# Dense stages of a four-layer graph network: LayerNorm statistics in five groups of five tiles instead of one pass, and the accumulators cleared by ScalarE instead of GpSimd

## The chip, the cores and the metric

The program runs on one core of one Trainium2 chip. The metric is the device time of one execution in microseconds (us), lower is better. A profile is one further execution, taken by the hardware profiler.

## The reference

Four residual layers on 3125 nodes with 256 features and 50000 edges. Each layer normalizes the rows of `x`, applies ReLU, and feeds the result to one layer kind:

```python
h = jnp.maximum(_layernorm(x, axis=-1), 0.0)
x = x + _L0_gnn_ref(h, edge_weight, src, dst)          # h @ (256x256 product of rotations)
h = jnp.maximum(_layernorm(x, axis=-1), 0.0)
x = x + _L1_gnn_ref(h, edge_index, edge_attr_64, ...)  # q, k, v, skip projections, edge softmax, sums by target
h = jnp.maximum(_layernorm(x, axis=-1), 0.0)
x = x + _L2_gnn_ref(h, edge_index, ...)                # GAT: h @ W0.T, scores, edge softmax, elu
h = jnp.maximum(_layernorm(x, axis=-1), 0.0)
x = x + _L3_gnn_ref(h, edge_index, edge_attr_64, ...)  # GAT block with a closing layernorm
```

`_layernorm` is `(x - m) / sqrt(v + 1e-5)` over the 256 features of a row.

## The kernel before

The nodes lie in 25 tiles of 125 rows (`P` = 125, `NT` = 25, `D` = 256). `X` holds all of `x` in SBUF, and `acc` (125 x 25 x 272 numbers, 6800 a partition) holds the sums that the edge stages add up by target node. The program is a row of stages, each a `phase` that ends in a barrier of all engines: constants, the list of rotations, the rotations, dense 0, the graph stage, dense 1, blend (edges of layer 1), dense 2, attend 2 and its end, dense 3, attend 3, final. Only `dense_phase` is changed; it runs four times, for layers 0 to 3. The profile calls the tiles of all four `d_...`.

A dense stage has two parts, in this order.

**Statistics.** VectorE (DVE) runs a loop over all 25 tiles: a `bn_stats` (L946) for each. In layer 2 (`settle=True`) two more instructions stand ahead of it for each tile, which divide the tile's sums in `acc` by their weights (L942) and add them to `X` (L944). Then seven small instructions turn the statistics of all 25 tiles at once into a variance (L950 to L956), ScalarE (ACT) takes one square root for all (L1009), and two more on DVE make `rstd` and `nb` (L958, L959), which release the rest by the semaphore `ready`.

**Products.** A loop over five groups of `U` = 5 tiles, the first of them peeled off (`peeled`). ACT writes the five normalized tiles `hn` (L1017), then copies each tile's transpose from PSUM to `ht` (L1022). TensorE (PE) transposes a tile (`turn`, L1033, two matmuls) and multiplies the tile before it by the weights (`multiply`, L1044: 256 columns in layer 0, 1024 in layer 1, 272 in layers 2 and 3); its order is turn 0, turn 1, product 0, turn 2, product 1, turn 3, product 2, turn 4, product 3, product 4. DVE moves each product out of PSUM (L970; L972 to L977; L980 to L987). SyncE stores the tables to HBM. ACT may not write `hn` of a tile before DVE has finished the same tile of the group before (`evac`); only layer 3 reads `hn` on DVE (L980).

GpSimd (POOL) clears `acc` with one `memset` of 6800 columns (L1003), in layer 2 after the last tile has been settled. Each engine runs its own instructions strictly in their order.

Of the kernel before, what the change touches and what calls it, by code (L numbers as in the profile page):

```python
# [13 lines left out]
ALU = mybir.AluOpType  # L14
# [3 lines left out]
P = 125  # L18
# [5 lines left out]
D = 256  # L24
# [51 lines left out]
def peeled(eng, count, body):  # L76

    body(0)
    with eng.Fori(1, count) as i:
        body(i)  # L80

# [826 lines left out]
def dense_phase(nc, con, layer, X, acc, ntab, weight, width, bias, tables, base=None, settle=False, loads=()):  # L908

    U = 5  # L910
    with phase(nc) as ph:
# [8 lines left out]
        inv = sb("inv", [P, NT, H]) if settle else None  # L920
        banks = -(-width // 512)
# [5 lines left out]
        cleared, lined, slanted, settled, brought = sem("cleared"), sem("lined"), sem("slanted"), sem("settled"), sem("brought")  # L927
        stores = 2 if layer == 1 else len(tables)
        with nc.Block() as block:
            @block.vector  # L930
            def _(dve):
                if settle:
# [5 lines left out]
                with dve.Fori(0, NT) as n:  # L938
                    x = X[:, bass.ds(n, 1), :].rearrange("p a d -> p (a d)")
                    if settle:  # L940
                        m = acc[:, bass.ds(n, 1), 0:MW].rearrange("p a (h c) -> p (a h) c", h=H)[:, :, 0:C]
                        dve.tensor_tensor(m, m, inv[:, bass.ds(n, 1), :].rearrange("p a h -> p (a h)").unsqueeze(2).to_broadcast([P, H, C]), ALU.mult).then_inc(settled, 1)  # L942
                        dve.wait_ge(settled, n * 2 + 3)
                        dve.tensor_tensor(x.rearrange("p (h c) -> p h c", h=H), x.rearrange("p (h c) -> p h c", h=H), m, ALU.add).then_inc(settled, 1)  # L944
                        dve.wait_ge(settled, n * 2 + 4)
                    dve.bn_stats(st[:, bass.ds(n, 1), :].rearrange("p a s -> p (a s)"), x).then_inc(dv, 1)  # L946
                dve.wait_ge(dv, NT)
                c = Tally(dve, dv, NT)
                me, mo = st[:, :, 1], st[:, :, 4]
                c.up(dve.tensor_tensor(mean[:], me, mo, ALU.add))  # L950
                c.up(dve.tensor_tensor(dif[:], me, mo, ALU.subtract))
                c.then(dve.tensor_tensor(var[:], st[:, :, 2], st[:, :, 5], ALU.add))
# [8 lines left out]
                def body(i):  # L961
                    for u in range(U):
# [3 lines left out]
                        if stores and not isinstance(i, int):  # L966
                            dve.wait_ge(stored[u], 16 * stores * i)
# [1135 lines left out]
```

## Time and profile before

| what | value |
|---|---|
| median of 3 runs | 3375.41 us (3375.38 to 3379.78) |
| time of the profiled execution | 3375.93 us |
| its span (first to last instruction) | 3374.2 us |
| PE, DVE, ACT, POOL busy | 75%, 69%, 50%, 46% of the span |
| mean granted clock of PE | 0.857 of full speed |

The time of the profiled execution is 1.7 us more than its span; what is said of the span holds for the time. Since all stages are kept apart by barriers, a stage's length counts whole, and the shares of the page, which are averages over stages with quite different limits, say little about the dense ones. They are read stage by stage.

### The profile page before, as it was taken

The numbers are of one execution on the slowest core, as the hardware profiler recorded it, in microseconds if no ns is written. First come the engines' busy times: TensorE is split into PE (matmuls) and PEld (weight loads), VectorE is DVE, ScalarE is ACT, GpSimd is POOL, SyncE is SP. The second block draws the span as 40 slices with busy tenths as digits, with TensorE's granted clock in tenths as the row PEclk, the third lists the DMA queues.
The fourth block names the chain that finished last, engine by engine and source line by source line (L and its number), as shares of the span: only waits on it lengthen the run. The fifth ranks groups of instructions, "written<-read, shape, count | busy, mean of one in ns | idle before, by whom it ended". The sixth has DMA issues, their size and how long they took to land. (4 is left out here: it accounts for less than half of the span.)

```text
span 3374.2 us, 57511 instructions
## 1 busy us (share of the span) xinstructions
PE 2535.7 (75%) x13060; PEld 1918.1 (57%) x13061; DVE 2319.7 (69%) x5727; ACT 1680.8 (50%) x4017; POOL 1550.9 (46%) x1759
## 2 busy tenths in 40 slices
PE   2999997357999999999995358888881368787870
PEld 1888886223666666666664246666660256666650
DVE  4888886464677787777775636766778547666677
ACT  1666664111454555545552246666661356666651
POOL 1333332101454555445551077777750177777740
PEclk9999998678999999999997767877785768888785
DMA  2100000213555556555651155555532255555521
GB/s 72 19 8 10 10 8 7 64 53 103 152 156 151 158 153 162 154 151 156 162 156 35 36 145 139 139 140 138 138 96 36 59 154 141 140 143 140 142 74 38
DMA packets 186285, 348.91 MB, mean 103 GB/s; under 512 B 74085, under 2 KB 116478, under 8 KB 185951
## 3 DMA queue, kind: packets, MB, share of 16 engines
q0 software_dynamic: 83520, 249.39, 29.0%
q1 hardware_dynamic: 102685, 98.62, 10.2%
q8 instruction: 30, 0.49, 0.1%
q14 instruction: 50, 0.41, 0.0%
HBM read 325.45 MB, written 22.44 MB: 103 GB/s over the span
## 5 line engine op out<-in xcount | busy, mean ns | idle before, releaser
L1626 POOL DMA_INDIRECT t_rows<-table_h,t_istage x896 | 853.5, 953 | 266.1 <-issue 247.1
L1212 POOL DMA_INDIRECT b_rows<-table_kv,b_istage x448 | 480.5, 1072 | 389.5 <-PE b_pso L1349 266.7
L1713 PE MATMUL t_pso<-t_rows,t_hot 125*125 125x272 f32 (+1 forms) x1792 | 588.1, 483 | 68.8 <-DVE t_rows L1752 30.5
L1713 PEld LDWEIGHTS t_pso<-t_rows,t_hot 125*125 125x125 f32 x1792 | 395.7, 232 | 164.5 <-issue 73.4
L1274 ACT COPY b_asked<-b_psq 125x512 f32<-125x512 f32 x224 | 131.1, 585 | 470.3 <-PE b_psq L1313 470.3
L1752 DVE TENSOR_TENSOR t_rows<-t_rows,t_psm 125x1056 f32<-125x1056 f32 x224 | 276.9, 1236 | 33.0 <-issue 32.9
L1699 PE MATMUL t_pss<-node_scores,t_hot_t 125*125 x1792 | 269.4, 281 | 33.5 <-ACT t_hot_t L1657 31.1
L1699 PEld LDWEIGHTS t_pss<-node_scores,t_hot_t 125*125 125x125 f32 x1792 | 263.7, 227 | 49.2 <-issue 43.7
L1664 ACT ACTIVATE t_hot<-con_iota,g_dstl 125x125 f32<-125x125 f32 x896 | 280.3, 384 | 0.0
L1762 DVE TENSOR_TENSOR acc<-acc,t_pso 125x272 f32 (+1 forms) x448 | 192.6, 430 | 114.7 <-DVE acc L1762 70.0
L1313 PE MATMUL b_psq<-queries,b_hot_t 125*125 x896 | 235.5, 386 | 43.9 <-issue 26.2
L1329 PE MATMUL b_psk<-b_rows,con_ident 125*125 125x256 f32 x896 | 257.9, 411 | 0.0
L1349 PE MATMUL b_pso<-b_rows,b_hot 125*125 125x264 f32 x896 | 239.1, 412 | 24.8 <-DVE b_rows L1428 24.5
L1406 DVE TENSOR_TENSOR b_rows<-b_psk,b_asked 125x1024 f32<-125x1024 f32 x112 | 136.5, 1218 | 150.5 <-ACT b_asked L1274 150.5
L1655 ACT ACTIVATE t_hot_t<-t_places,t_minus 125x500 f32<-125x500 bf16 x224 | 156.5, 699 | 142.2 <-PE t_pss L1699 110.3
L1033 PE MATMUL d_pst<-con_ident,d_hn 125*128 125x125 f32 x200 | 37.9, 290 | 224.5 <-ACT d_hn L1017 224.5
L1313 PEld LDWEIGHTS b_psq<-queries,b_hot_t 125*125 125x125 f32 x896 | 162.7, 189 | 74.8 <-issue 50.9
L1329 PEld LDWEIGHTS b_psk<-b_rows,con_ident 125*125 125x125 f32 x896 | 152.5, 190 | 90.2 <-issue 77.0
L1349 PEld LDWEIGHTS b_pso<-b_rows,b_hot 125*125 125x125 f32 x896 | 165.2, 194 | 56.6 <-issue 28.9
L1326 PE MATMUL b_psk<-we,b_attr 64*125 64x256 f32 x896 | 160.4, 435 | 22.2 <-DMA b_rows<-table_kv,b_istage 14.5
L1044 PE MATMUL d_pso<-wt,d_ht 128*125 128x512 f32 (+1 forms) x400 | 150.8, 518 | 25.5 <-ACT d_ht L1022 25.5
L1033 PEld LDWEIGHTS d_pst<-con_ident,d_hn 125*128 125x128 f32 x200 | 28.1, 151 | 245.2 <-ACT d_hn L1017 227.0
(392 smaller groups left out, 5194.3 us busy)
## 6 DMA issues: line engine op xcount, KB each, us to landing
t_places<-targets SPq DMA_DIRECT2D x56, 488.3 KB
t_rows<-table_h,t_istage POOLq DMA_INDIRECT x896, 3.0
b_attr<-in_attr_t SPq DMA_DIRECT2D x224, 62.5 KB
b_places<-targets SPq DMA_DIRECT2D x28, 488.3 KB
b_rows<-table_kv,b_istage POOLq DMA_INDIRECT x448, 5.2
table_h<-d_stage SPq DMA_DIRECT2D x50, 132.8 KB
t_flag<-flags SPq DMA_DIRECT2D x56, 62.5 KB
table_kv<-d_moved SPq DMA_DIRECT2D x25, 128.9 KB
```

Source lines behind the costliest of these rows:

```text
L1212: pool.indirect_dma_start(out=rows[:, h, s, :], out_offset=None, in_=table, in_offset=bass.IndirectOffsetOnAxis(ap=istage[:, h, s:s + 1], ...
L1313: mm = pe.matmul(ps_q[0:P, w * D:(w + 1) * D], hot_t[:, b % 2, v * PAIR + w, :], q, start=True, stop=True)
L1326: pe.matmul(to(v * PAIR + w), attr[half, b, w * P:(w + 1) * P], we[half], start=True, stop=False)
L1329: mm = pe.matmul(to(u), ident[0:P, 0:P], rows[0:P, h, b * G + u, 0:D], start=False, stop=True)
L1349: mm = pe.matmul(ps_o[0:P, at:at + MW], hot[:, h, b * G + u, :], rows[0:P, h, b * G + u, D:WIDE], start=u % PAIR == 0, stop=u % PAIR == PA ...
L1626: pool.indirect_dma_start(out=rows[:, r, s, :], out_offset=None, in_=table, in_offset=bass.IndirectOffsetOnAxis(ap=istage[:, r, s:s + 1], ...
L1655: act.activation(x, places[:, r, b * G * P:(b + 1) * G * P], ACT.Abs, bias=minus[0:P, :]).then_inc(broad, 1)
L1664: act.activation(hot[:, r, b * G + u, :], con["iota"][0:P, 0:P], ACT.Abs, scale=-1.0, bias=g["dstl"][:, bass.ds(n * G + u, 1)]).then_inc(d ...
L1699: mm = pe.matmul(expanded[:, b * G + u], hot_t[:, b % 2, u, :], ntab[:, bass.ds(ts[u // PAIR], 1), 0:nw].rearrange("p a d -> p (a d)"), st ...
L1713: mm = pe.matmul(ps_o[b % 2][0:P, at:at + mw], hot[:, r, b * G + u, :], rows[0:P, r, b * G + u, 0:mw], start=u % PAIR == 0, stop=u % PAIR ...
L1752: dve.tensor_tensor(v, v, weight[:, b * G:(b + 1) * G].unsqueeze(3).to_broadcast([P, G, H, HW]), ALU.mult).then_inc(mset, 1)
L1762: dve.tensor_tensor(row, row, ps_o[b % 2][0:P, v * 512:v * 512 + mw], ALU.add).then_inc(added, 1)
```

## The change

The statistics are taken group by group. On DVE `measure(g)` holds the five `bn_stats` of a group (in layer 2 with their two instructions of settling) and the seven small instructions, now over 5 columns instead of 25; `level(g)` holds the two that follow the square root. DVE runs `measure(0)` and `level(0)` ahead of the loop. In the loop, group `i` begins with `measure(i + 1)`, then finishes its tile 0, then `level(i + 1)`, then tiles 1 to 4. ACT takes the square root of group `i + 1` (`root`) between its second and third copy of group `i`. The wait of ACT on `evac` ahead of `hn` stays in layer 3 alone. POOL clears a small tile `zeros` (1360 columns) at the start, and ACT copies it over the group's five tiles of `acc` (`clear`) at the end of each group. The last group is peeled off as well on DVE and ACT (`tapered`).

```diff
+def tapered(eng, count, body):
+    body(0)
+    with eng.Fori(1, count - 1) as i:
+        body(i)
+    body(count - 1)
...
+                def measure(g):
+                    c = Tally(dve, dv, g * PER)
+                    for u in range(U):
...
+                        c.up(dve.bn_stats(st[:, bass.ds(n, 1), :].rearrange("p a s -> p (a s)"), x))
...
+                    dve.tensor_scalar(var[:, s], var[:, s], EPS, None, ALU.add).then_inc(spread, 1)
...
+                def body(i):
+                    if not last(i):
+                        measure(i + 1)
+                    finish(i, 0)
+                    if not last(i):
+                        level(i + 1)
+                    for u in range(1, U):
+                        finish(i, u)
...
-                with dve.Fori(0, NT) as n:
...
-                dve.wait_ge(ready, 1)
-                peeled(dve, NT // U, body)
+                measure(0)
+                level(0)
+                tapered(dve, GROUPS, body)
...
-                    if settle:
-                        pool_wait(pool, settled, 2 * NT + 2)
-                    pool.memset(acc[:], 0.0).then_inc(cleared, 1)
-                    pool.wait_ge(cleared, 1)
+                    pool.memset(zeros[:], 0.0).then_inc(empty, 1)
+                    pool.wait_ge(empty, 1)
...
+                def root(g):
+                    s = bass.ds(g * U, U)
+                    act.wait_ge(spread, g + 1)
+                    act.activation(dif[:, s], var[:, s], ACT.Sqrt).then_inc(rooted, 1)
+
+                def clear(g):
+
+                    act.copy(acc[:, bass.ds(g * U, U), :].rearrange("p n x -> p (n x)"), zeros[:].rearrange("p n x -> p (n x)")).then_inc(cleared, 1)
...
                 def body(i):
+                    act.wait_ge(ready, i + 1)
                     for u in range(U):
                         n = i * U + u
-                        if not isinstance(i, int):
+                        if layer == 3 and not opening(i):
                             act.wait_ge(evac, n - U + 1)
...
+                    copied(i, 0)
+                    copied(i, 1)
+                    if not last(i):
+                        root(i + 1)
+                    for u in range(2, U):
+                        copied(i, u)
+                    if layer:
+                        clear(i)
```

What stands on ACT in the first, peeled group of layer 1, before (the square root of all tiles, the five normalized tiles, the five copies of transposes, then the loop's branch):

```order
L1009 ACTIVATE d_dif<-d_var 125x25
L1017 ACTIVATE d_hn<-x,d_nb,d_rstd 125x256 x5
L1022 COPY d_ht<-d_pst 128x250 x5
L79 UNCONDITIONAL_BRANCH
L79 ISA
```

And what stands there in the changed kernel:

```order
L1062 ACTIVATE d_hn<-x,d_nb,d_rstd 125x256 x5
L1054 COPY d_ht<-d_pst 128x250 x2
L1046 ACTIVATE d_dif<-d_var 125x5
L1054 COPY d_ht<-d_pst 128x250 x3
L1050 COPY acc<-d_zeros 125x1360
```

The square root of the next group stands between the second and the third copy of this one, and the copy of zeros between the fifth copy and the next group's `hn`. The table for the square root is loaded once ahead of each dense stage in both kernels.

What stands on DVE at the start of the first group of layer 2, before (end of the statistics of all tiles, then tile 0 and the start of tile 1 of the group):

```order
L956 TENSOR_SCALAR d_var<-d_var 125x25
L958 RECIPROCAL d_rstd<-d_dif 125x25
L959 SCALAR_TENSOR_TENSOR d_nb<-d_mean,d_rstd 125x25
L991 MEMSET d_stage 125x5x8
L981 COPY node_scores<-d_pso 125x8
L982 COPY d_stage<-d_pso 125x8
L985 TENSOR_TENSOR node_scores<-d_pso,d_stage 125x8
L987 COPY d_stage<-d_pso 125x8x32
L981 COPY node_scores<-d_pso 125x8
```

And in the changed kernel, from the last tile that `measure(1)` settles to the start of tile 1:

```order
L960 TENSOR_TENSOR acc<-acc,d_inv 125x8x32
L962 TENSOR_TENSOR x<-x,acc 125x256
L964 BN_STATS d_st<-x 125x6
L968 TENSOR_TENSOR d_mean<-d_st 125x5
L969 TENSOR_TENSOR d_dif<-d_st 125x5
L970 TENSOR_TENSOR d_var<-d_st 125x5
L971 TENSOR_SCALAR d_mean<-d_mean 125x5
L972 SCALAR_TENSOR_TENSOR d_dif<-d_dif 125x5
L973 SCALAR_TENSOR_TENSOR d_var<-d_var,d_dif 125x5
L974 TENSOR_SCALAR d_var<-d_var 125x5
L1002 COPY node_scores<-d_pso 125x8
L1003 COPY d_stage<-d_pso 125x8
```

Four more such triples stand ahead of the first row. The statistics of the next group are now in front of tile 0 of this one, and the `MEMSET` of `d_stage` stands ahead of `measure(0)`.

## Rows read from the trace of the kernel before

**Rows 1.** The page: span.

```profile
span 3374.2 us, 57511 instructions
```

**Rows 2.** Windows: the products of layers 0, 1; statistics and products of 2; products of 3.

```profile
core 0: us, PE busy (x) PEld busy (x) DVE busy (x) ACT busy (x) POOL busy (x), PEclk, DMA share, GB/s
...
580.97:618.95 37.98, 30.42 (x150) 24.45 (x150) 10.54 (x25) 21.18 (x50) 0.00 (x0) 0.92 0.00 0
...
710.22:818.97 108.75, 96.61 (x250) 43.49 (x250) 54.81 (x101) 21.74 (x50) 0.00 (x0) 0.96 0.18 58
1846.92:1896.69 49.77, 0.00 (x0) 0.00 (x0) 40.02 (x87) 1.47 (x2) 5.76 (x1) 0.50 0.03 10
1896.69:1939.93 43.24, 33.24 (x150) 25.13 (x150) 18.72 (x102) 21.75 (x50) 0.00 (x0) 0.91 0.24 71
...
2641.23:2684.36 43.13, 33.15 (x150) 24.92 (x150) 22.70 (x101) 21.75 (x50) 0.00 (x0) 0.92 0.23 70
```

**Rows 3.** Timeline of layer 1's statistics: start us, us, engine, line, operation.

```profile
695.91 12.25 DVE L946 BATCH_NORM_STATS2 d_st<-x  x25 [2.96 <-PEq L73]
708.19 0.20 DVE L950 TENSOR_TENSOR d_mean<-d_st 125x25 f32<-125x25 f32 x1
...
709.18 0.18 DVE L956 TENSOR_SCALAR d_var<-d_var 125x25 f32<-125x25 f32 x1
...
710.22 2.56 ACT L1017 ACTIVATE d_hn<-x,d_nb,d_rstd 125x256 f32<-125x256 f32 x5 [0.60 <-DVE d_nb L959]
```

**Rows 4.** Layer 2's 25 settling instructions (ns, first and last start).

```profile
L942 DVE TENSOR_TENSOR acc<-acc,d_inv x25: 425/425/426, 1849.2 to 1888.5; - x25
```

**Rows 5.** Timeline of layer 2's clearing of acc on POOL and DVE beside it.

```profile
1889.57 5.76 POOL L1003 MEMSET acc<- 125x6800 f32 x1 [102.12 <-DVE x L944]
...
1890.52 4.85 DVE L953 TENSOR_SCALAR d_mean<-d_mean 125x25 f32<-125x25 f32 x1
```

**Rows 6.** Timeline of one group of layer 0; brackets: idle before, releaser.

```profile
596.12 2.62 ACT L1017 ACTIVATE d_hn<-x,d_nb,d_rstd 125x256 f32 x5
...
597.50 0.42 DVE L970 TENSOR_TENSOR x<-x,d_pso 125x256 f32 x1 [0.44 <-PE d_pso L1044]
598.65 0.61 ACT L1022 COPY d_ht<-d_pst 128x250 f32<-128x250 f32 x2
...
599.13 1.12 PE L1044 MATMUL d_pso<-MT,d_ht 128*125 128x256 f32 x4 [1.35 <-ACT d_ht L1022]
...
600.50 0.37 ACT L1022 COPY d_ht<-d_pst 128x250 f32<-128x250 f32 x1 [1.24 <-PE d_pst L1033]
...
603.12 2.63 ACT L1017 ACTIVATE d_hn<-x,d_nb,d_rstd 125x256 f32 x5
```

**Rows 7.** Timeline of layer 1: where a group's first product begins, two groups.

```profile
773.74 0.59 PE L1033 MATMUL d_pst<-con_ident,d_hn 125*128 125x125 f32 x4
...
776.37 3.69 PE L1044 MATMUL d_pso<-wt,d_ht 128*125 128x512 f32 x8 [2.04 <-ACT d_ht L1022]
...
796.93 5.39 PE L1044 MATMUL d_pso<-wt,d_ht 128*125 128x512 f32 x8 [2.04 <-ACT d_ht L1022]
```

**Rows 8.** Timeline of layer 2: its first product, and the last group's start.

```profile
1899.56 2.18 PE L1044 MATMUL d_pso<-wt,d_ht 128*125 128x272 f32 x4 [1.04 <-ACT d_ht L1022]
...
1929.41 2.29 ACT L1017 ACTIVATE d_hn<-x,d_nb,d_rstd 125x256 f32 x4
```

**Rows 9.** Timeline of layer 3, around the start of one group.

```profile
2657.70 0.37 ACT L1022 COPY d_ht<-d_pst 128x250 f32<-128x250 f32 x1 [0.95 <-PE d_pst L1033]
...
2660.14 0.41 DVE L987 COPY d_stage<-d_pso 125x256 f32<-125x256 f32 x1
...
2661.29 0.61 ACT L1022 COPY d_ht<-d_pst 128x250 f32<-128x250 f32 x2
2661.76 1.18 PE L1044 MATMUL d_pso<-wt,d_ht 128*125 128x272 f32 x4 [1.83 <-ACT d_ht L1022]
```

**Rows 10.** ACT's groups by form: busy us, mean ns, idle before and releaser.

```profile
L1274 ACT COPY b_asked<-b_psq 125x512 f32<-125x512 f32 x224 | 131.1, 585 | 470.3 <-PE b_psq L1313 470.3
...
L1022 ACT COPY d_ht<-d_pst 128x250 f32<-128x250 f32 x100 | 34.3, 363 | 103.5 <-PE d_pst L1033 103.5
```

More of the change, by code:

```diff
@@ L910, in dense_phase @@
     U = 5
+    GROUPS = NT // U
     with phase(nc) as ph:
@@ L920, in dense_phase @@
         inv = sb("inv", [P, NT, H]) if settle else None
+        zeros = sb("zeros", [P, U, RW]) if layer else None
         banks = -(-width // 512)
@@ L926, in dense_phase, with last @@
         stored = [sem(f"stored{u}") for u in range(U)]
-        cleared, lined, slanted, settled, brought = sem("cleared"), sem("lined"), sem("slanted"), sem("settled"), sem("brought")
+        empty, cleared, lined, slanted, settled, brought, put = (
+            sem(n) for n in ("empty", "cleared", "lined", "slanted", "settled", "brought", "put"))
         stores = 2 if layer == 1 else len(tables)
+        def last(i):
+            return isinstance(i, int) and i == GROUPS - 1
         with nc.Block() as block:
@@ L937, in _ @@
                     dve.wait_ge(con["x_brought"], 16)
-                with dve.Fori(0, NT) as n:
-                    x = X[:, bass.ds(n, 1), :].rearrange("p a d -> p (a d)")
-                    if settle:
[L941 to L952, printed above, removed]
-                c.up(dve.tensor_scalar(mean[:], mean[:], 0.5, None, ALU.mult))
-                c.then(dve.scalar_tensor_tensor(dif[:], dif[:], 0.25, dif[:], ALU.mult, ALU.mult))
@@ L1018, in body @@
                                        bias=nb[:, bass.ds(n, 1)], scale=rstd[:, bass.ds(n, 1)]).then_inc(hset, 1)
-                    for u in range(U):
-                        n = i * U + u
-                        act.wait_ge(tset, n + 1)
-                        act.copy(ht[:, u], ps_t[u % 2][:, 0:2 * P].rearrange("p (a m) -> p a m", a=2)).then_inc(tcopied, 1)
-                peeled(act, NT // U, body)
+                    copied(i, 0)
[6 more added lines that the diff above has]
+                        clear(i)
+                root(0)
+                if layer:
+                    act.wait_ge(empty, 1)
+                tapered(act, GROUPS, body)
             @block.tensor
@@ L1070, in body @@
                                 sp.dma_start(tables[0][bass.ds(n * P, P), :], stage[:, u, :]).then_inc(stored[u], 16)
-                    peeled(sp, NT // U, body)
+                    peeled(sp, GROUPS, body)
                     for u in range(U):
-                        sp.wait_ge(stored[u], 16 * stores * (NT // U))
+                        sp.wait_ge(stored[u], 16 * stores * GROUPS)
                     if loads:
```

93 lines of the change are left out of this document (55 added, 38 removed).

## The prediction

> **What bounds the kernel now.** I read the page first for the span of 3374.2 us [rows 1], then a table of windows over the dense stages [rows 2], then the timeline inside them. The stages stand behind one another with barriers between, so what a dense stage gets shorter, the whole gets shorter. A dense stage has two parts that never overlap. In the statistics only DVE works: in layer 1 they last from 695.91 to 710.22, 14.3 us [rows 3], and in layers 0 and 3 the same length (the pattern repeats three times); in layer 2, where each tile is settled as well, 49.8 us with no matmul at all [rows 2]. In the products PE is busy 89% of layer 1's 108.75 us, so PE bounds that one, and 77 to 80% in the others, where nobody is full: DVE has 10.5 of 38.0 us in layer 0, 18.7 of 43.2 in layer 2, 22.7 of 43.1 in layer 3 [rows 2]. There the round through ACT bounds: five `hn`, two copies, PE's first product, the third copy behind it [rows 6].
>
> **What is taken off the front.** One `bn_stats` takes 0.49 us (12.28 us for 25, from 695.91 to 708.19), and from there to the first `hn` it is 2.03 us [rows 3]. With 5 columns instead of 25 I take 1.85 for the latter (an estimate, bounds 1.6 and 2.03). A group's statistics then cost 5 x 0.49 + 1.85 = 4.3 us, and the first `hn` comes 10.0 us earlier in layers 0, 1 and 3. In layer 2 a tile costs 1.64 us (39.3 us over 24 steps [rows 4]), 20 tiles 32.7 us. There POOL's clearing of `acc` also held a DVE `TENSOR_SCALAR` for 4.85 us, to the end of the 5.76 us memset [rows 5], where it takes 0.18 otherwise [rows 3]; that 4.7 us goes too, and with the 0.2 of narrower columns it makes 37.6 us.
>
> Against it: the new clearing of `zeros` is a fifth as wide, 5.76 x 1360/6800 = 1.15 us, and begins with the stage, while DVE now begins layers 1 and 3 with its own memset, and layer 2 with a `TENSOR_SCALAR`, the form that was held. I charge 0.8 us in each of the three (bounds 0 and 1.15; for the memset no row shows it). Front: -10.0 - 9.2 - 36.8 - 9.2 = **-65.2 us**.
>
> **What comes back in the products.** The seven small instructions of `measure` took 1.2 us up to the release of the root [rows 3]; in the loop their waits stand against registers, for which I add 0.25. A slice is then 5 x 0.49 + 1.45 = 3.9 us, and 5 x 1.64 + 1.45 = 9.65 in layer 2 (bounds 0.3 less, 0.6 more). Four slices run in each layer. DVE has room for them, but ACT's square root waits for the slice, and the third, fourth and fifth copies of the group ahead are queued behind it; PE's products 2 to 4 wait for those, and DVE's finishing of them. The first slice of layers 0, 1 and 3 begins with the first `hn` and is done ahead of the third copy.
>
> *Layer 0.* Count from an `hn` start, T = 596.12 [rows 6]. DVE finishes the group before at T + 1.8; the slice ends at T + 5.7. The third copy, at T + 4.4 before, comes at T + 6.15. Its product follows 0.48 later (598.65 to 599.13) and the fifth copy 1.37 behind that product's start (599.13 to 600.50), T + 8.0, the next `hn` at T + 8.45, against 7.0. Three groups pay 1.45: **+4.35**, net -5.65.
>
> *Layer 1.* PE's transposes begin at 773.74 and the first product at 776.37, because ACT's `hn` of tiles 3 and 4 waited on DVE by `evac`. Without that wait `hn` is ready long before, and the product follows transpose and copy by 0.42 + 0.48 = 0.9 us instead of 2.63 [rows 7]: -1.73 in four rounds, -6.9. One of these rounds met half the clock after the 2.04 us of idle and took 5.39 instead of 3.69 us [rows 7]; I take that 1.7 as saved as well. The slice is hidden: DVE needs 54.81/25 = 2.2 us a tile [rows 2], 11 and 4.9 for slice and level, of 18.8 us a round. So is the clearing, which ACT does while PE multiplies. **-8.6**, net -17.8.
>
> *Layer 2.* The slice of 9.65 us is longer than the round, which was (1929.41 - 1896.69)/4 = 8.2 us [rows 2, 8]. Count from the end of a slice, M. Root and third copy follow at M + 0.45, the product at M + 0.9, and DVE has finished tile 4 at M + 5.3 if PE runs at full clock (1.18 us a product [rows 9]). But PE has then idled some 6 us, and a gap of 2 us was already enough once for half the clock [rows 7]. At the lower level a product takes 2.18 [rows 8], the three and the transpose between end 3.1 us later, M + 8.4. Then the next slice. A round is 18.05 us (14.95 at full clock). I take the lower level for all rounds but the first. From the first `hn`: 9.4 (first slice) + 5.3 + 9.65 = 24.3, two rounds make 60.4; from the end of the last slice to the last `hn` 5.45 (fifth copy at M + 3.6, clearing, start), and from there 10.0 (10.5 before [rows 2, 8], without the wait on `evac`). 75.8 us against 43.2 [rows 2]: **+32.6**, net -4.2.
>
> The Trainium skill, TensorE: Matmul & The Clock Gate, section HAM oscillation, says that a loop whose bursts of matmuls are separated by long enough waits restarts every burst at the lower clock. This speaks against the change in layer 2. The trace agrees by the 5.39 us product; with the rule left out layer 2 would be the full-clock case.
>
> *Layer 3.* The wait on `evac` stays. The clearing is a copy of 1360 columns: the rows have 363 ns for 250 and 585 for 512 columns [rows 10], 0.85 ns a column, so 1.3 us, with start 1.35 (bounds 1.1 and 1.6). Count from the fifth copy, C = 2657.70 [rows 9]. The first copy of the next group stood at C + 3.6, now at C + 0.45 + 1.35 + 2.6 = C + 4.4. DVE finishes at C + 2.85, the slice ends at C + 6.75, the third copy comes at C + 7.2 and the fifth at C + 9.05, a round, against 7.9. With tile 4 finishing 0.35 later, the next two rounds pay 1.45. 1.15 + 2 x 1.45 + 0.8 for the last group: **+4.9**, net -4.3.
>
> The Trainium skill, ScalarE: Activation LUTs, section Rules for kernel authors, budgets 0.3 us plus 0.83 ns an element, which would make the clearing an estimated 1.43 us. By it layer 3 would pay a few tenths more.
>
> Sum: -5.65 - 17.8 - 4.2 - 4.3 = -31.95 us, on the profiled execution's own 3375.93: 3344.0. The median of the runs is 0.5 lower: **3343.5 us**.
>
> **The rivals.**
> 1. *Layer 2 keeps the full clock* (0.20). Rounds of 14.95: 24.3 + 29.9 + 4.2 + 10.0 = 68.4, 7.4 us less: 3336. For it: in layers 0, 2 and 3 gaps of 1.4 and 1.8 us left the clock alone [rows 6, 9]. Against: 6 us is three times longer than any gap inside a round today.
> 2. *The held root costs nothing in layers 0 and 3* (0.08), if the slices run shorter than I have them: 4.35 + 4.05 less, 3335. Against: the third copy is due at T + 4.4 and DVE has only 2.6 us ahead of it.
> 3. *Slices are dearer* (0.09): a dozen instructions and more, some with waits on registers, 1.5 us more in each of the nine that count: 3357.
> 4. *Slower: the lower clock spreads* (0.03). The root's wait opens a second gap in each round of layers 0 and 3, and if PE drops there and in layer 1 as well, 40 tiles pay about 1.0 us (2.18 less 1.18) and 20 pay 1.7 [rows 7 to 9]: +74, 3417. It decides from 19 of layer 1's 20 tiles on. Against: these gaps are 1 to 2 us, and layer 1's becomes shorter.
> 5. *No change* (0.05): the front is taken off but the stage's end is set by something not in my rows, such as the stores of the tables, and the time stays within 0.2% of 3375.4. Against: DMA is busy 0.18 to 0.24 in the products [rows 2].
>
> My forecast has 0.55, with a range of its own of 3338 to 3350.
>
> **How the numbers follow.** Low end: rival 1 with clearing and memsets free, 3331. High end: slices at 0.6 more in nine places (+5.4), the collision at its full 1.15 (+1), half clock once more in layer 1 (+1.7) and in a few tiles of layer 3 (+4): 3356. A measurement of this kernel can tell about 0.2%, 6.8 us, from no change. All but rivals 4 and 5 lie below 3368.6: faster 0.92, the same 0.05, slower 0.03.
>
> **What would show it.** First `hn` 4.3 us after the first `bn_stats` in layers 0, 1 and 3, and some 10.4 after the division in layer 2. ACT's square root waiting 2 to 3 us for DVE in layers 0 and 3 and about 8 in layer 2, with the third copy right behind it. Products in layer 1 18.8 us a round, no wait of ACT on DVE. In layer 2 rounds of 18 us, products of 2.1 us at half clock behind the gap. A copy of zeros of 1.3 us. Wrong would make it: rounds in layer 2 over 20 us, DVE held by POOL for more than a microsecond, or gaps between the instructions of a slice.

## The result and the profile after

The changed kernel takes 3328.9 us (median of 4 runs, 3326.4 to 3330.5); the kernel before, run beside it, 3377.6 us. The ratio is 0.9856, 95% interval 0.9844 to 0.9868: 48.7 us faster, where I had forecast 32 us, with 3331 as the low end of the range. One execution of the kernel e7 below took 6150.0 us; it is left out of e7's ratio, and nothing on record says why it took that long. The profiled execution of after took 3328.8 us. Its page begins:

```profile
span 3327.0 us, 57408 instructions
```

That is 47.2 us under [rows 1]. Windows over the dense stages of after (columns as in [rows 2]): the products of layers 0 and 1, the first statistics of layer 2, the products of layers 2 and 3.

```profile
570.25:610.45 40.20, 31.69 (x150) 24.85 (x150) 22.48 (x81) 20.90 (x54) 0.00 (x0) 0.92 0.00 1
690.23:790.39 100.16, 94.91 (x250) 42.86 (x250) 66.14 (x156) 27.53 (x59) 0.00 (x0) 0.97 0.20 63
1823.70:1833.79 10.09, 0.00 (x0) 0.00 (x0) 9.18 (x28) 1.45 (x2) 1.19 (x1) 0.50 0.15 52
1833.79:1902.93 69.14, 40.74 (x150) 29.49 (x150) 47.12 (x197) 26.61 (x59) 0.00 (x0) 0.76 0.15 44
2590.61:2636.99 46.38, 36.29 (x150) 25.56 (x150) 34.09 (x156) 27.14 (x59) 0.00 (x0) 0.89 0.22 65
```

Set against [rows 2, 3] they give the table that the rest of this text uses, in us. "Front" is first DVE instruction to first `hn`, "products" from there to DVE's last instruction; a stage's front before is 14.3 in layers 0, 1 and 3.

| layer | front, forecast | front, measured | products, forecast | products, measured | net, forecast | net, measured |
|---|---|---|---|---|---|---|
| 0 | -10.0 | -10.9 | +4.35 | +2.2 | -5.65 | -8.6 |
| 1 | -9.2 | -10.8 | -8.6 | -8.6 | -17.8 | -19.4 |
| 2 | -36.8 | -39.7 | +32.6 | +25.9 | -4.2 | -13.8 |
| 3 | -9.2 | -10.8 | +4.9 | +3.3 | -4.3 | -7.6 |
| sum | -65.2 | -72.2 | +33.25 | +22.8 | -31.95 | -49.4 |

The other stages give back 2.2 us, which makes the 47.2. Most of that is in the stages that gather rows of a table for every edge (blend behind dense 1, attend 2 behind dense 2; "gather stages" from here on, each counted from the last DVE instruction of one dense stage to the first of the next): that of layer 1 is 5.4 longer, that of layer 2 is 2.8 shorter.

The timeline of layer 1's first group shows most of what was mis-sized. The rows answer to [rows 3, 5].

```profile
686.63 1.23 POOL L1038 MEMSET d_zeros<- 125x1360 f32 x1 [56.12 <-POOLq L73]
686.72 0.41 DVE L964 BATCH_NORM_STATS2 d_st<-x 125x6 f32<-125x256 f32 x1 [2.70 <-PEq L73]
686.74 0.09 DVE L1027 MEMSET d_moved<- 125x40 f32 x1
...
689.50 0.21 ACT L1046 ACTIVATE d_dif<-d_var 125x5 f32<-125x5 f32 x1 [80.83 <-DVE d_var L974]
...
690.04 1.73 DVE L964 BATCH_NORM_STATS2 d_st<-x 125x6 f32<-125x256 f32 x5
690.23 2.08 ACT L1062 ACTIVATE d_hn<-x,d_nb,d_rstd 125x256 f32<-125x256 f32 x4 [0.52 <-DVE d_nb L981]
```

Five `bn_stats` take 1.73 us, 0.35 each and not 0.49; and DVE's memset of `moved` takes 0.09 us beside POOL's memset, so nothing collides.

Layer 2, PE and then ACT, in one middle group of after: the slice of statistics ends at 1871.2.

```profile
1863.55 0.38 PE L1085 MATMUL d_pst<-con_ident,d_hn 125*128 125x125 f32 x2
1863.76 1.08 PE L1096 MATMUL d_pso<-wt,d_ht 128*125 128x272 f32 x4
1864.68 0.38 PE L1085 MATMUL d_pst<-con_ident,d_hn 125*128 125x125 f32 x2
1872.38 2.15 PE L1096 MATMUL d_pso<-wt,d_ht 128*125 128x272 f32 x4 [7.33 <-DVE d_stage L1008]
```

```profile
1871.35 0.21 ACT L1046 ACTIVATE d_dif<-d_var  x1 [8.68 <-DVE d_var L974]
1871.46 0.62 ACT L1054 COPY d_ht<-d_pst 128x250 f32<-128x250 f32 x2
...
1875.25 1.33 ACT L1050 COPY acc<-d_zeros 125x1360 f32 x1
```

ACT's root waits 8.7 us with the third copy right behind it, PE stands 7.3 us, and the product behind the gap takes 2.15 us instead of 1.08. But the bracket names DVE's `finish`, not ACT's copy: there is a second hold, of which the prediction knew nothing.

### The profile page after: what moved, and what is told of

Read it like the earlier page. It is cut to its first block and busy times, and to the rows that moved or that the text cites. A ratio compares the mean times of both kernels' runs of the same rounds, so it can differ in the third digit from the quotient of the medians.

```text
span 3327.0 us, 57408 instructions
## 1 busy us (share of the span) xinstructions
PE 2562.3 (77%) x13060; PEld 1934.9 (58%) x13061; DVE 2325.5 (70%) x5871; ACT 1696.8 (51%) x4048; POOL 1537.8 (46%) x1759
## 3 DMA queue, kind: packets, MB, share of 16 engines
q1 hardware_dynamic: 102685, 98.62, 10.3%
## 5 line engine op out<-in xcount | busy, mean ns | idle before, releaser
L1765 PE MATMUL t_pso<-t_rows,t_hot 125*125 125x272 f32 (+1 forms) x1792 | 601.3, 492 | 72.7 <-DVE t_rows L1804 35.4
L1765 PEld LDWEIGHTS t_pso<-t_rows,t_hot 125*125 125x125 f32 x1792 | 404.5, 237 | 171.4 <-issue 74.5
L1720 ACT ACTIVATE t_hot<-t_hot,con_ones 125x500 f32<-125x500 f32 x224 | 159.4, 712 | 7.3
L1709 ACT ACTIVATE t_hot_t<-t_hot_t,con_ones 125x500 f32<-125x500 f32 x224 | 159.4, 712 | 7.3
```

The lines of the kernel that those rows point to most:

```text
L1709: act.activation(x, x, ACT.Relu, scale=-1.0, bias=con["ones"][0:P, 0:1]).then_inc(hot_ts, 1)
L1765: mm = pe.matmul(ps_o[b % 2][0:P, at:at + mw], hot[:, r, b * G + u, :], rows[0:P, r, b * G + u, 0:mw], start=u % PAIR == 0, stop=u % PAIR ...
```

## The experiments

Runs e1 to e8 were made on two chips on which the gather stages are slower (the kernel before takes 3688 and 3693 us there) and the dense stages the same; so ratios and the rows of dense stages are compared, not the whole times. The changed kernel was not run on these two; 48.7 us less of some 3690 would be a ratio of 0.987 (an estimate). Rounds are from the first `hn` of one group to that of the next.

**e1: the pitch of a loop.** The kernel before with one edit:

```
-                with dve.Fori(0, NT) as n:
+                for n in range(NT):
```

> The kernel before, with its 25-pass loop of statistics written out instead of looped, nothing else changed. Theory A (part of the gain is only that bn_stats no longer stands in a one-instruction loop: 0.49 us a pass in the loop, 0.35 written out in the changed kernel; in layer 2 1.64 against 1.25 a tile): 25 x 0.14 = 3.5 us less in layers 0, 1 and 3 each, 25 x 0.39 = 9.8 less in layer 2, 20 us in all, some 3357 us, and bn_stats 0.35 us apart. Rival (the pitch is shorter because the slices lie beside other work, or because the groups are small): bn_stats stays 0.49 us apart and the time stays within 3 us of before.

Ratio 0.9935 (0.9915 to 0.9956). The fronts are 10.33, 10.31, 39.98 and 10.31 us, 21.8 us less in all, and the products of the four layers together 1.1 us less. Layer 1's:

```profile
691.72 8.25 DVE L946 BATCH_NORM_STATS2 d_st<-x 125x6 f32<-125x256 f32 x25 [2.65 <-PEq L73]
```

25 `bn_stats` take 8.25 us, 0.33 each, where the one-instruction hardware loop needed 12.25 [rows 3]. So 0.16 us of each pass was the loop's. In layer 2 a tile falls from 1.64 to 1.25. Writing the loop out thus gives 21.8 us with no overlap at all, against the 49.4 us of the whole change in the dense stages.

**e2: who clears.** The changed kernel, with `acc` cleared by POOL in one memset as before.

```
-                    pool.memset(zeros[:], 0.0).then_inc(empty, 1)
+                    pool.memset(acc[:], 0.0).then_inc(cleared, 1)
...
-                    if layer:
-                        clear(i)
```

> The changed kernel, but POOL clears acc with one memset of 6800 columns as before and ACT copies no zeros. Theory B (the copy of zeros costs 0.8 us a round in layer 3 alone, and POOL's memset holds those DVE instructions that it held before): layer 3's rounds 0.6 to 0.8 us shorter, but in layers 1 and 3 the first TENSOR_SCALAR of the statistics is held until the memset ends, some 3.5 us each, and in layer 2 about 4 us in the last slice; in all 6 to 9 us slower than the changed kernel, about 3336. Rival (the memset holds nothing that matters, the move to ScalarE is a loss): 3 us faster than the changed kernel, 3326.

Ratio 0.989 (0.987 to 0.991), against the estimate of 0.987 for the changed kernel, which the interval just reaches; the rows tell more. Layer 1's first group:

```profile
686.15 5.76 POOL L1040 MEMSET acc<- 125x6800 f32 x1 [56.89 <-POOLq L73]
...
688.15 0.16 DVE L970 TENSOR_TENSOR d_var<-d_st 125x5 f32<-125x5 f32 x1
688.35 3.60 DVE L971 TENSOR_SCALAR d_mean<-d_mean 125x5 f32<-125x5 f32 x1
688.42 3.52 DVE L972 SCALAR_TENSOR_TENSOR d_dif<-d_dif 125x5 f32<-125x5 f32 x1
```

Beside the memset the `TENSOR_TENSOR` and `bn_stats` run on, the `TENSOR_SCALAR` of 5 columns stands until it ends. The `SCALAR_TENSOR_TENSOR` queued behind it ends at the same time, so these rows do not show whether the memset would have held it by itself. The front is 6.83 us instead of 3.51 in layers 1 and 3; the last round of layer 2 is 20.98 instead of 16.93. What the change does with `zeros` is therefore worth 3.3 + 3.3 + 4.1 us at these three places. (Layer 2's products as a whole are 72.4 us against 69.1, since the first round is 1.1 shorter here, 9.6 against 10.6.) Layer 3's last three rounds are 8.56, 8.53 and 8.28 without ACT's copy of zeros and 8.54, 8.56 at full clock with it: the 0.8 us a round that I had added for it was not there in the middle rounds, and is at most 0.3 us in the last.

**e3: the wait on `evac`,** put back in layers 0 to 2.

```
-                        if layer == 3 and not opening(i):
+                        if not opening(i):
```

> The changed kernel with ACT's wait on evac ahead of hn in all layers, as before. Theory C (all that layer 1's products gained is that this wait is gone): layer 1's rounds go from 18.8 back to 20.5 us, 7 us slower in all, about 3336, layers 0 and 2 unchanged within 1 us because ACT there starts hn after DVE has finished, or the slice bounds. Rival (the gain in layer 1's products comes from elsewhere, such as the clock): layer 1's rounds stay 18.8.

Layer 1's rounds are 20.56 us instead of 18.83, 1.73 as forecast; layer 0's do not move (7.72), the last two of layer 2 are 16.2 and 16.6 instead of 16.9. Ratio 0.9887 (0.9856 to 0.9919), too wide by itself. Layer 3, which this edit doesn't touch, has three rounds of 9.8 us here where the first trace of after has one of 9.81 and two of 8.55; changed_again and e11 take that up.

**e4: TensorE kept busy in layer 2** by idle products in the gap, into a spare bank (PE's last group is peeled off for it, so that only the middle groups have them).

```
+                        if layer == 2 and u == 3 and not isinstance(i, int):
+                            for _ in range(20):
+                                pe.matmul(ps_w[0:P, 0:width], ident[:, 0:P], weight[:, 0, 0:width], start=True, stop=True)
```

> The changed kernel with 20 extra products of 272 columns into a spare PSUM bank, never read, in front of the third product of layer 2's three middle groups, so that PE works while DVE settles the next group (5.4 us at full clock, in a gap of 5.6 to 7.4 us). Theory D (the gap costs half the clock for the third to fifth product, and DVE's finishing of them bounds the round): third product 1.1 instead of 2.15 us, rounds of layer 2 from 16.9 to 14 or 14.5 us, 7 us faster, about 3322. Rival (the round is bound by DVE alone and the clock there is worth nothing): rounds stay 16.9, time within 2 us of the changed kernel.

```profile
1895.88 9.33 PE L1105 MATMUL d_psw<-wt,con_ident 128*125 128x272 f32 x40
1905.04 1.08 PE L1097 MATMUL d_pso<-wt,d_ht 128*125 128x272 f32 x4
```

The third product runs at full clock (1.08 us), but 20 idle products take 9.3 us, 0.47 each, and overrun the gap: rounds of 17.3 instead of 16.9, ratio 0.9886 (0.9859 to 0.9912). Inconclusive for the price; repeated as e9.

**e5, e6, e7: which hold?** Two waits end right behind the slice: ACT's root, with the third copy queued behind it, and DVE's `finish(i, 0)`, which PE's third product waits for. e5 issues the root behind the fifth copy:

```
-                    copied(i, 0)
-                    copied(i, 1)
+                    for u in range(U):
+                        copied(i, u)
                     if not last(i):
                         root(i + 1)
-                    for u in range(2, U):
-                        copied(i, u)
```

with `level(i + 1)` behind `finish(i, 2)`; e6 changes what the third product waits for; e7 does both.

```
-                        pe.wait_ge(evac, n - 2 if u >= 3 else n - 1)
+                        pe.wait_ge(evac, n - 2 if u >= 3 else n - 4 if u == 2 else n - 1)
```

> The changed kernel with ScalarE's square root issued behind the fifth copy of a group instead of behind the second, and VectorE's level moved from behind finish(i, 0) to behind finish(i, 2), so that no copy is queued behind the root. Theory R (what the prediction said: ScalarE's held root is what stretches a round, since the third copy stands behind it): rounds fall to those of the kernel before, layer 0 7.0 us instead of 7.7, layer 3 7.9 us instead of 8.5, layer 2 from 16.9 us to about 14.5; about 13 us less in all, some 0.4% of the whole, so the ratio to the kernel before comes out near 0.982. Theory D (a second hold just as long: TensorE's third product of a group waits for VectorE's finish(i, 0), which stands behind the slice of statistics, since multiply waits for evac n - 1 at u = 2 too, though the bank it needs was emptied in the group before): the root alone brings almost nothing, layer 0 7.4 to 7.7, layer 2 16.0 to 16.9, ratio 0.985 to 0.987.

> The changed kernel with one number of multiply's wait changed: at u = 2 it waits for evac n - 4 (the tile that last used the bank, of the group before) instead of n - 1 (tile 0 of its own group, which VectorE finishes behind the slice). Theory R: no gain, since the third copy is still queued behind the held root: layer 0 7.7, layer 2 16.9, ratio as the changed kernel, 0.986 or a little over. Theory D as the only hold: the third product starts before the slice ends, rounds of layer 2 fall by 2 us or more, ratio 0.982. Both holds (what I now expect): no gain from either alone, gaps of the third product end with its copy instead of with the finish.

> Both edits: the root behind the fifth copy, level behind finish(i, 2), and evac n - 4 at u = 2. The three products of a group that have banks then run while VectorE measures. If both holds are needed, only this one shows the gain: layer 0 rounds 7.0 to 7.2 us, layer 3 7.9 to 8.1, layer 1 as before 18.8; layer 2 is then VectorE's own sum, 8.8 us of the slice, 5 x 0.9 us of finishing and 0.6 us of level, 14.0 us, or up to 15.5 us if TensorE's fourth product falls to the low clock after its wait for finish(i, 0). In all 9 to 13 us less than the changed kernel, ratio near 0.982. If theory R alone is right it equals the run with the root alone; if something else bounds the rounds (the low clock, the count of banks) it stays at 16 us and more in layer 2.

| kernel | layer 2, last three rounds | layer 2, products | layer 0, middle rounds | ratio |
|---|---|---|---|---|
| changed | 15.2, 16.9, 16.9 | 69.1 | 7.7, 7.7 | 0.9858 |
| e5 | 15.2, 17.3, 17.2 | 69.0 | 9.5, 7.8 | 0.9895 |
| e6 | 14.7, 16.1, 16.6 | 68.2 | 7.8, 7.8 | 0.9885 |
| e7 | 13.2, 13.8, 15.0 | 61.4 | 7.8, 7.8 | 0.9884 |

(The changed kernel's row is from faster chips, and its ratio would be some 0.987 on the slower one; the others' intervals are 0.002 to 0.003 wide to either side.) PE's third product in layer 2 in e5, then in e6:

```profile
1901.82 2.15 PE L1095 MATMUL d_pso<-wt,d_ht 128*125 128x272 f32 x4 [7.68 <-DVE d_stage L1008]
```

```profile
1899.20 2.17 PE L1096 MATMUL d_pso<-wt,d_ht 128*125 128x272 f32 x4 [6.54 <-ACT d_ht L1054]
```

With the root out of the way, DVE's `finish(i, 0)` holds it; with that wait gone, the copy behind the root does. Neither edit alone gives more than 1 us over the stage, both together 7.7: two holds of nearly the same length. The wait for `evac n - 1` at `u = 2` is stricter than the bank needs, which was last used by tile 2 of the group before. In the short rounds of layers 0 and 3 nothing is won: layer 0 stays at 7.8 and pays 9.3 to 9.5 in a round or two that falls to the low clock, and layer 3 has rounds of 9.9. My expected 7.0 and 7.9 were wrong.

For layer 0 the rows of ACT show why, and it is the edit's own doing. In a middle group of the changed kernel, and then of e7:

```profile
578.92 2.57 ACT L1062 ACTIVATE d_hn<-x,d_nb,d_rstd 125x256 f32 x5
...
584.22 0.21 ACT L1046 ACTIVATE d_dif<-d_var  x1 [2.23 <-DVE d_var L974]
584.34 0.62 ACT L1054 COPY d_ht<-d_pst 128x250 f32<-128x250 f32 x2
```

```profile
582.07 2.57 ACT L1063 ACTIVATE d_hn<-x,d_nb,d_rstd 125x256 f32 x5 [0.68 <-DVE d_nb L981]
...
586.40 0.37 ACT L1055 COPY d_ht<-d_pst 128x250 f32<-128x250 f32 x1 [1.25 <-PE d_pst L1084]
...
588.82 0.21 ACT L1047 ACTIVATE d_dif<-d_var  x1
589.86 2.57 ACT L1063 ACTIVATE d_hn<-x,d_nb,d_rstd 125x256 f32 x5 [0.83 <-DVE d_nb L981]
```

The third copy comes 5.4 us behind the start of `hn` in the changed kernel, and 4.3 in e7, where it stood before the change (4.4 [rows 6]). But in e7 the root stands at the end of the group, and the next `hn` waits 0.83 us for what DVE makes of it. One wait has been traded for another, so e5 and e7 do not show what a round costs with the root free. In layer 2 of e7 the next `hn` waits for it too (1.6 and 1.8 us), and the two edits together still take 7.7 us off the stage.

**e8: the slice woven between the finishing of tiles,** in all layers, with the five groups written out in place of the hardware loop, and with both edits of e7. `gauge` is the settling and `bn_stats` of the tiles named, the seven small instructions of `measure` are `spreads`.

```
+                    gauge(i + 1, range(3))
                     finish(i, 0)
+                    gauge(i + 1, [3])
+                    finish(i, 1)
+                    gauge(i + 1, [4])
+                    spreads(i + 1)
+                    finish(i, 2)
+                    level(i + 1)
+                    finish(i, 3)
+                    finish(i, 4)
```

> Both edits of the run before, and the slice is woven between the finishing of tiles (three tiles of the next group measured, finish 0, a tile, finish 1, a tile and the spread, finish 2, level, finish 3 and 4), with all five groups of each stage written out on VectorE and ScalarE instead of three of them in a hardware loop. Theory (VectorE's own work bounds layer 2, at 1.25 us a settled tile written out as against 1.46 in the loop, and products that come one by one keep TensorE's full clock): layer 2 rounds 12.5 to 13.5 us, layer 0 7.0, layer 3 7.9; some 18 to 22 us less than the changed kernel, ratio near 0.980. Rival (the time from level to the first finish, 3.5 us, is no longer covered by the slice, or the order holds TensorE elsewhere): layer 2 at 15 us or over, no better than the run before.

Layer 2's rounds are 11.5, 11.8 and 11.4 us, below what I expected, its products 58.9 us instead of 69.1. Layers 0 and 3 pay for it (42.7 and 50.8 us, with rounds of 9.1, 10.3 and 11.3), and the ratio is 0.9889 (0.9868 to 0.9910).

The changed kernel was then run again, with the next three on its chip.

> The changed kernel itself, as the measure for its variants on the same chip. If its gain is that of the dense stages (49.4 us of them, 2.3 us given back elsewhere), the ratio stands near 0.9865 here too, a little higher than 0.9856 since the same microseconds are a smaller share of a longer kernel: 0.987. Layer 3's rounds: theory G (TensorE's clock in this stage stands at an edge and falls in some rounds whatever the code) at least one round of 9.8 us among the four; if all the 9.8 us rounds of the variants came from their edits, one at most, as in the first trace of the changed kernel.

3331.8 us, ratio 0.9858 (0.9842 to 0.9874): the first result again. Its dense stages agree with the first trace within 0.3 us, but for layer 3: products 48.5 us against 46.4, because two rounds are 9.8 us, not one, and the first is 11.1, not 10.1. So the 9.8 us rounds, which are at the low clock, come without any edit.

**e9: 13 idle products** in place of e4's 20.

> As the run that kept TensorE busy with 20 idle products in layer 2's middle groups, with 13 of them (13 x 0.47 = 6.1 us against gaps of 7.3 us): they end before the slice does. Theory (the low clock behind the gap costs 1 us on the third product and some on those around it): the third product takes 1.08 us instead of 2.15, and rounds of layer 2 are 14.5 to 15.5 us instead of 16.9. Rival (the round is held by finish(i, 0) and by the root, both behind the slice, and the low clock is only part of it): 15.9 us, the 1.07 us of one product.

```profile
1864.77 6.12 PE L1105 MATMUL d_psw<-wt,con_ident 128*125 128x272 f32 x26
1871.06 1.15 PE L1097 MATMUL d_pso<-wt,d_ht 128*125 128x272 f32 x4 [0.17 <-DVE d_stage L1009]
```

The idle products end before the slice does, the granted clock stays at its full level, and the last two rounds are 14.5 us instead of 16.9. The low clock is thus worth 2.4 us in each of these. The round ahead of them is 0.6 longer (15.8 against 15.2), so that the stage's products are 66.5 us against 69.1; the whole moves by less than can be told (0.9857, 0.9840 to 0.9874).

**e10, e11: woven in layer 2 alone** (the order, the waits and the written-out groups of e8 there, the changed kernel elsewhere); e11 adds two idle products in each group of layers 0 and 3, where PE waits for ACT's copy.

```
+                        if layer in (0, 3) and u == 1:
+                            for _ in range(2):
+                                pe.matmul(ps_w[0:P, 0:width], ident[:, 0:P], weight[:, 0, 0:width], start=True, stop=True)
```

> The changed kernel with the woven order, the root last, evac n - 4 at u = 2 and the five groups written out in layer 2 alone; the other layers as in the changed kernel. Expected: layer 2 at 69.0 us as in the woven run, 10.2 us under the changed kernel's 79.2, layers 0, 1 and 3 as in the changed kernel, so 10 us less than the changed kernel and a ratio near 0.984. If the gain of layer 2 is given back by what stands behind it (the stores of the table, the clock of layer 3), the ratio stays at the changed kernel's.

> The run before with two idle products (0.9 us at full clock) between the second transpose and the first product of each group of layers 0 and 3, where TensorE waits 1.4 us for ScalarE's copy. Theory G (the clock falls in bursts in these stages since TensorE waits 1.7 us of each round; an extra 0.9 us of work keeps it up): every round of layer 3 at 8.5 us, none at 9.8, and layer 0 at 7.7; up to 4 us less than the run before. Rival (the bursts come from elsewhere, or the idle products are themselves in the way): 9.8 us rounds remain, or 8.9 us and over.

e10 has layer 2's products at 55.9 us, 13.2 less than the changed kernel's, and is not faster: 0.9863 (0.9846 to 0.9879). e11 has 0.9874 (0.9858 to 0.9891), though all its rounds of layer 3 are at full clock (8.43, 8.61, 8.59) and the stage's products take 45.2 us. That is what theory G forecast, but it does not prove it: e2 has no round at the low clock in layer 3 either (all its last three at a granted clock of 1.00), without idle products and with longer waits of PE, 1.7 and 1.8 us; nor have e15 and e17 below (8.7 to 8.8 us). What sets the clock there is open. The gain of layer 2 goes elsewhere: the gather stage behind it takes 702.4 and 702.9 us in these two, 684.2 and 685.6 in the changed kernel's traces, and what stands behind layer 3 694.1 and 696.9 against 690.1 and 690.3.

**e12, e13, e14: where it goes.** e12 is e10 with layer 2's middle groups in the hardware loop again; e13 is the changed kernel, with only layer 2's groups written out; e14 is e10 once more.

```
-                (written if layer == 2 else tapered)(dve, GROUPS, body)
+                tapered(dve, GROUPS, body)
```

> The woven layer 2 as before, but its middle three groups in the hardware loop again, as in the changed kernel. Theory K (the 17 us that the following gather stage lost in the two woven runs on the last chip come from the code written out): layer 2 about 62 us (1 us a round more, register addresses), the gather stage behind it 685 us again, ratio 0.981 to 0.982. Theory S (they come from the order itself, or from the point at which that stage starts): the stage takes 700 us again and the ratio stays near 0.986.

> The changed kernel, with nothing but layer 2's five groups written out on VectorE and ScalarE, in the changed kernel's order. Theory K: layer 2 at 75 us instead of 79, but the gather stage behind it 700 us, ratio 0.989 to 0.990. Theory S: the gather stage 685 us, ratio 0.985.

> The kernel of the woven layer 2 once more (written out), to see whether the 702 us of the gather stage behind it is a property of the kernel. If it is, 700 us again and a ratio near 0.986; if it was the chance of one execution (theory N: the gather stage's clock settles differently from run to run), 684 to 690 us and a ratio near 0.982.

| kernel | layer 2, products | gather stage behind | time | ratio |
|---|---|---|---|---|
| changed again | 69.1 | 685.6 | 3331.8 | 0.9858 |
| e12 | 64.2 | 685.0 | 3321.7 | 0.9837 (0.9820 to 0.9853) |
| e13 | 62.4 | 698.2 | 3341.4 | 0.9893 (0.9876 to 0.9909) |
| e14 | 57.6 | 704.1 | 3335.1 | 0.9872 (0.9856 to 0.9889) |

The written-out code loses it, not the order: e13 has the changed kernel's order and loses 13 us there, e12 has the woven order in a loop and loses nothing. DVE's waits in the gather stage (engine, line, releaser: us in total, times, longest) in e12 and in e14; "issue" is time in which the engine waited for nothing that the profile shows:

```profile
DVE t_rows L1880 <- issue: 37.1, 28, 1.8
```

```profile
DVE t_rows L1880 <- issue: 69.8, 28, 8.1
```

e12 has the lowest median of this study (3319.6 to 3322.6 us in four runs; the changed kernel took 3328.7 to 3336.0 on another chip, and the intervals of the two ratios overlap).

**e15, e16, e17: place or amount?** e12 with 64, 128 or 192 memsets of one column of a spare tile ahead of layer 2's statistics, which push DVE's later code back and lengthen layer 2's front by 1.8, 3.6 and 7.1 us. One run each, on one chip: 3340.8, 3323.9 and 3354.6 us.

```
+                if layer == 2:
+                    for k in range(64):
+                        dve.memset(spare[:, k:k + 1], 0.0)
```

> The woven layer 2 in loops, with 64 tiny memsets of a spare tile at the start of layer 2 on VectorE, which only move all of VectorE's later code by 64 instructions (and cost some 5 us of VectorE there). Theory P (the stall ahead of one instruction of the gather stage's loop comes from where the loop stands in VectorE's code): at one or more of the three shifts (64, 128, 192) that wait grows from 37 us with at most 1.8 us at a time to about 70 us with up to 8 us, and the gather stage behind layer 2 takes 698 to 705 us instead of 685; at others it stays. Theory Q (it comes from the amount of code that layer 2 has, or from the order of its work): 37 us and 685 us at all three, or growing steadily with the shift. The Trainium skill, Runtime: NRT & Kernel Launch, section Instruction fetch mechanics, says that an engine's instructions come in blocks of 256 and that a taken branch to a block that is not held stalls until it is loaded, which would be theory P.

> As the run with 64 memsets, with 128 (some 9 us of VectorE). Theory P: the wait is 37 us or 70 us, by where the loop now stands, and not in proportion to the shift. Theory Q: 37 us, or twice what 64 added.

> As the run with 64 memsets, with 192 (some 14 us of VectorE). Theory P: 37 us or 70 us by place; if the wait is back at 37 us here after 70 us at a smaller shift, the amount of code is ruled out. Theory Q: 37 us at all three, or three times what 64 added.

DVE's waits in the gather stage behind layer 2 in e15, e16 and e17:

```profile
DVE t_rows L1884 <- issue: 76.8, 28, 9.1
```

```profile
DVE t_rows L1884 <- issue: 36.8, 28, 1.8
```

```profile
DVE t_rows L1884 <- issue: 75.2, 28, 8.8
```

The stage takes 703.8, 685.8 and 704.4 us. It is the place of the loop in DVE's code, not the amount: 64 more instructions cost this stage 19 us against e12's 685.0, 128 cost 1. The page's queue of instructions tells the same (queue, kind: packets, MB, share), here e16 and then e15:

```profile
q14 instruction: 56, 0.45, 0.0%
```

```profile
q14 instruction: 84, 0.69, 0.1%
```

28 packets more, as many as the loop's 28 waits. The same 84 or 85 packets stand on the pages of e10, e11, e13, e14 and e17, and 50 to 56 on all others. (The wait alone does not tell: on the two slower chips it is 48 to 61 us with 51 to 55 packets, in e8 too, whose code is written out in all layers.) The Trainium skill, Runtime: NRT & Kernel Launch, section Instruction fetch mechanics, says that an engine's instructions come in blocks of 256, and that a taken branch into a block that isn't held stalls until it is loaded. The trace agrees as far as it goes: an extra packet for each of 28 stalls of up to 9 us, there at two shifts of four. Why the long and the short stalls alternate at steps of 64 instructions does not follow from that, and no run here shows it. The section also says that kernels prefer loops written out in full where possible; by e13 that is dear here, since written-out code moves a loop that comes later.

## Why the prediction was wrong

**The step that failed** is "One `bn_stats` takes 0.49 us (12.28 us for 25)", and with it "in layer 2 a tile costs 1.64 us". Both were pitches of a hardware loop of one and three instructions, and I took them for the instructions'. Written out they are 0.33 and 1.25 us (e1), and a settled tile takes 1.46 inside the loop over groups. With bounds of "0.3 less, 0.6 more" a slice, the range shut out what happened. A slice measures 3.2 us instead of 3.9, and in layer 2 8.9 in the loop (7.4 ahead of it) instead of 9.65. Of the 17.4 us that the dense stages gained beyond the forecast, the fronts carry 0.7 x 3 + 0.13 x 3 + 5 x (1.64 - 1.25) = 4.4 us by the pitch (0.7 is 5 x 0.14 of `bn_stats`, 0.13 the small instructions, which were shorter too), and the four slices of layer 2's products some 4.5.

**The collision** with POOL, charged at 0.8 us in three stages, is 0: 2.4 us more. DVE's first instruction of layer 2 (a `TENSOR_SCALAR` of 200 columns) runs in 0.48 us beside POOL's memset, the memset of layer 1 in 0.09. The row that I had leaned on, 4.85 us beside the memset [rows 5], was of another instruction, and e2 shows that one held again; what sets the two `TENSOR_SCALAR`s apart is open (both are f32; one is strided out of `acc`).

**Layer 0, +4.35, was +2.2.** The middle rounds are 7.72 us instead of 8.45. The mechanism is the one forecast: the root waits 2.2 us, with the third copy right behind it at 5.4 us from the start of `hn`; the slice, 0.7 shorter than I had it, puts it there and not at 6.15. No run here frees the root without adding a wait of its own.

**Layer 1, -8.6, is -8.6,** by its own terms: from the first `hn` to the last group's first product it is 79.8 us where it was 86.7, 6.9 less, and from there to the end 20.3 where it was 22.0. e3 gives the 1.73 us a round back. Root and slice are hidden, as said; the sign that I had named, no wait of ACT on DVE, did not come: ACT waits 4.6 us a round, at no cost.

**Layer 2, +32.6, was +25.9.** The mechanism is the one forecast: one group waits for the slice, and PE falls to the lower clock behind it. Over a middle group of after, windows of 4, 2 and 2 us, with the granted clock as the third number from the end:

```profile
1872.00:1876.00 4.00, 3.62 (x9) 2.80 (x10) 1.97 (x11) 1.09 (x3) 0.00 (x0) 0.50 0.20 60
1876.00:1878.00 2.00, 2.00 (x7) 1.43 (x6) 0.74 (x4) 2.00 (x5) 0.00 (x0) 0.65 0.22 65
1878.00:1880.00 2.00, 1.07 (x8) 0.76 (x7) 1.34 (x6) 1.55 (x5) 0.00 (x0) 1.00 0.22 71
```

The lower clock costs 2.4 us in each of the last two rounds (e9), where I had 3.1. Of the 6.7 us that I was off, some 4.5 is the slices, the rest this and the last group (9.5 us, forecast 10.0). The HAM oscillation of the Trainium skill, TensorE: Matmul & The Clock Gate, which I had weighed against the full-clock case, is borne out by these rows. What I had missed is the second hold, DVE's `finish(i, 0)` behind the slice, through a wait of PE that is stricter than its bank needs (e5 to e7).

**Layer 3, +4.9, was +3.3.** Copy of zeros 1.33 us, forecast 1.35; but it costs the middle rounds nothing (e2), so most of the 0.8 falls away, and the slice is shorter. Against it stand rounds of 9.81 us at the low clock, one to three of a stage's last three, and one in the first run of the changed kernel but two in the second. e11, with idle products, has none; nor have e2, e15 and e17, without them. Without the one in the first run the stage would stand at +2.0: that +3.3 lies near the forecast is in part luck.

**The gather stages** I took as fixed. They are, for the change as it stands (+2.2 us in all); the 5.4 us that layer 1's got longer is open, and that stage takes 1025.5 us in e16 and 1034.0 in e17, which do not differ ahead of its end. That layer 2's stayed was luck of the place: e13 writes the same code out, two groups more, and loses 13 us.

**The rivals.** The nearest is number 2 by its time (3335), and only half by its reason: the slices are shorter, but the held root still costs layer 0 some 0.7 us a round. Number 1 did not happen (layer 2 does fall to the lower clock), though the low end of my range took its 7.4 us. That the whole came out below even that has one main cause: all my cases were worked out with the same pitch, which carries 8.9 of the 17.4 us in the fronts and in layer 2 and most of what layers 0 and 3 came out lower.

## What to carry to other kernels

Take an instruction's cost from a place where it stands behind others of its kind, never from the passes of a loop of one instruction; where only the loop is there, its pitch is an upper bound, and the range has to reach below it. Where work is put ahead of others' results on an engine, list every wait that now ends behind it, those for banks too: removing one of two equal holds shows next to nothing, and moving a wait can put what follows from it on the path. And when a stage's gain doesn't reach the end, compare the "issue" waits of the loops that come later and the packets of the instruction queues: the edit may have moved these loops in the code.

## What the runs showed of the hardware that I had not expected

- A pass of a one-instruction hardware loop on DVE costs 0.49 us where the instruction written out takes 0.33 to 0.35.
- The place of a loop in DVE's code decides whether its 28 passes stall 37 us in all (longest 1.8) or 75 to 77 (longest 9.1), which is 19 us of the stage: 64 or 192 instructions more, long; 0 or 128 more, short. One run each.
- POOL's memset of 6800 columns holds DVE's `TENSOR_SCALAR` on 5 columns for 3.6 us (and what is queued behind it), while `bn_stats` and `TENSOR_TENSOR` run on; its memset of 1360 columns held neither a DVE memset nor a `TENSOR_SCALAR` on 200 columns.
- With the same gaps of 1.4 us in each round of layer 3, the changed kernel has one of its last three rounds at the lower clock (9.8 us, granted clock 0.83) in one run and two in another; e15 and e17, with these gaps too, have none.
